# Second layer of a two-layer attention and expert kernel: the last group's expert rows scaled, added and put into statistics one batch per turn, its query block and the two blocks behind it one turn later

## The chip, the cores and the metric

One Trainium2 chip, one core. The metric is device time in microseconds (us) of one launch. The time before is 733.93 us, the median of 3 runs (733.39 to 734.78).

## What is computed

The input `x` is 16 batches of 112 tokens with 256 features, the context 375 rows of 256 features per batch. Two layers follow one another, each of cross attention and a feed-forward part, each part on a layer norm of `x` and added to `x`:

```
x = x + _L0_xattn_ref(_layernorm(x), ctx, ctx, mask, ...)   # one head, masked, own layer norm
x = x + _L0_ffn_ref(_layernorm(x), ...)                     # top 2 of 8 experts and 2 shared ones
x = x + _L1_xattn_ref(_layernorm(x), ctx, ctx, Wq, Wk, Wv, Wo)
x = x + _L1_ffn_ref(_layernorm(x), W, b, V_r, C)            # x @ (W + C V_r^T) + b
```

`_L1_xattn_ref` has 16 heads of 16 features:

```
scores = jnp.einsum('bhqd,bhkd->bhqk', q, k) * scale
attn = jax.nn.softmax(scores, axis=-1)
ctx = jnp.einsum('bhqk,bhkd->bhqd', attn, v)
return ctx.transpose(0, 2, 1, 3).reshape(...) @ Wo.T
```

## The kernel before

The 16 batches are four groups `i` of four batches `j`. The first layer's attention and shared experts come first, then 35 tiles of 128 expert rows (up to about 516 us), then the second layer. The result of the experts lies in DRAM (`yscr`). For each batch the two rows of every token are gathered into `yg[:, j, k, :]` (`gather`, L1857, indirect DMA issued by GpSimd), weighted and added to `x_res`. Then come layer norm statistics (`row_stats`, `rows_joined`), the reciprocal root (`rstd_of`) and the normalized rows `xh`, of which the second layer's queries are made. Groups 0 to 2 go through this beside the expert tiles. The last group, 3, can be gathered only after the last tile, and goes through it inside the second layer's attention.

That attention runs in **turns** `b` = 0 to 14, written out by hand in `tensor`, `vector`, `scalar`, `gpsimd` and `sync` of `second_layer`, and a tail for batch 15. Turn `b` of TensorE computes, for batch `b`, the transposed scores in four quarters `q` of four heads, each in three chunks `k` of keys (`transposed`, L2371), and the product with the values (`outputs`, L2380). It also computes the plain scores of batch `b + 2`, eight pairs `g` of heads (`scores`, L2351), which serve only for the row maxima. The engines' shares of a turn are:

- VectorE: eight reductions (`maximum`, L1996), one per pair. Two of them (`g` = 0, 1) come first, then the heads of batch `b - 1` (`finish`, L2008, L2010), the copy of the transposed maxima of `b + 1` (`turned`, L2002), then `g` = 2 to 7. Scores use two pairs of PSUM banks in turn, so `scores(b, g)` waits until `maximum` has read the pair before the last one (`EARLIER`, `pair_read`).
- ScalarE: `keep_outputs(b - 1)` (L2208) and twelve exponentials (`exps`, L2204), three per quarter. `transposed(b, q + 1)` waits for the exponentials of quarter `q`, chunk by chunk, since they read its banks. `outputs` wait for them too.
- GpSimd: `parted(b)` (L1769 to L1775) splits the maxima of batch `b` into three bf16 parts. TensorE transposes them (`maxima_T`, L2356) in turn `b - 1`.
- SyncE: keys, values and the rows of maxima by DMA.

Some turns carry a **block** of the other work (`BLOCKS`): `q` the queries of group 3, `o` the output projection of a group and its residual and statistics, `f` the feed-forward product. A block of `q` and `f` needs its group normalized. GpSimd does that (`rstd_of`, `normalized_beside`, L1839 to L1847), between two `parted`.

For group 3 before the change: ScalarE scales the eight rows of `yg` in turns 2 and 3 (`scaled`, L2199, four in each turn). GpSimd adds them (`combine`, L1880), two batches and then two. VectorE does the four `bn_stats` (L1917) and four `bn_aggr` (L1928, L1930) in one go in turn 4, behind `turned(5)`. The `q` block stands in turn 5, `o` of group 0 in turn 6 and `f` of group 0 in turn 8. Turns 7, 9, 11 and 14 have no block.

Of the kernel before, what the change touches and what calls it, by code (L numbers as in the profile page):

```python
# [22 lines left out]
G = 4  # L23
NG = B // G
# [1593 lines left out]
def second_layer(nc, tensors, first, routed, dram, out, x_res, weight1, weight2, slots, mhalf, ps, bank, ident, new_semaphore, pool_semaphore):  # L1618
# [29 lines left out]
    EARLY = NG - 1  # L1648


    BLOCKS = {5: ("q", 3), 6: ("o", 0), 8: ("f", 0), 10: ("o", 1), 12: ("f", 1), 13: ("o", 2), 15: ("f", 2)}
    NORMALIZED = {4: ("q", 3), 7: ("f", 0), 11: ("f", 1), 14: ("f", 2)}

    def blocks_in(b):
        return BLOCKS.get(b, (None, None))

# [39 lines left out]
    def pair_bank(use, k):  # L1696
        return bank[2 * PAIR[use] + k]
# [49 lines left out]
    def split_queries(eng, i):  # L1747

        eng.wait_ge(s["q1_ready"], (i + 1) * C)
        if i:  # L1750
            eng.wait_ge(s["q_out"], i * 16)
        eng.tensor_copy(qa[:, 1, :, :], qr[:]).then_inc(s["q2_ready"], 1)
        eng.wait_ge(s["q2_ready"], 3 * i + 1)
        eng.tensor_tensor(qr[:], qr[:], qa[:, 1, :, :], ALU.subtract).then_inc(s["q2_ready"], 1)
# [117 lines left out]
    def gpsimd(pool, n):  # L1872

        def combine(i, js):
            for j in js:
                for k in range(2):
                    pool.wait_ge(s["scaled"], 2 * j + k + 1)
                    if k:
                        pool.wait_ge(s["added"], 2 * j + k)
                    pool.tensor_tensor(x_res[:, i * G + j, :], x_res[:, i * G + j, :], yg[:, j, k, :], ALU.add).then_inc(s["added"], 1)  # L1880

        ones_below(pool, 1)
        ones_below(pool, 2)
        ones_below(pool, 3)
        pool.memset(va[:, :, :, :, HD:HD + 1], 1.0).then_inc(s["va_ready"], 1)
        pool.wait_ge(s["va_ready"], 2)
        zeros_below(pool, 1)
        pool.wait_ge(s["m_ready"], 4)
        split_queries(pool, EARLY - 1)
        split_rest(pool, EARLY - 1)  # L1890
        i = NG - 1
        for j in range(G):
            if j % 2:
                parted(pool, j // 2 + 2)
            pool.wait_ge(s["p_ready"], (2 * j + 2) * NKC)
            gather(pool, i, j)
        for j in range(0, G, 2):
            combine(i, range(j, j + 2))
            parted(pool, j // 2 + 4)
        rstd_of(pool, n, NORMS["q", i])  # L1900
        normalized_beside(pool, i, NORMS["q", i])
        parted(pool, 6)
        parted(pool, 7)
        split_queries(pool, i)
        split_rest(pool, i)
        for i, batches in enumerate(((8,), (9, 10, 11, 12), (13, 14, 15))):
            for b in batches:
                parted(pool, b)
            rstd_of(pool, n, NORMS["f", i])
            normalized_beside(pool, i, NORMS["f", i])  # L1910
            add_bias(pool, i)
        i = NG - 1
        rstd_of(pool, n, NORMS["f", i], AHEAD)
# [6 lines left out]
    def mean_var(v, n, i, js=slice(0, G)):  # L1920
        row_stats(v, n, i, js)
        rows_joined(v, n, js)
# [65 lines left out]
    def vector(v, n):  # L1988
# [71 lines left out]

        for b in range(B - 1):
            what, i = blocks_in(b)
            kind, k = NORMALIZED.get(b, (None, None))
            ahead_of = b + 2 < B
            if ahead_of:
                maximum(b + 2, 0)
                maximum(b + 2, 1)
            if b:
                finish(b - 1)
            turned(b + 1)  # L2070
            if kind == "q":
                v.wait_ge(s["added"], 2 * G)
                mean_var(v, n, k)
            if ahead_of:
                for g in range(2, 5):
                    maximum(b + 2, g)
            if ahead_of:
                maximum(b + 2, 5)
                maximum(b + 2, 6)
            if what == "o":  # L2080
                attended(i, slice(0, 2))
                v.wait_ge(s["x3_ready"], i * G + 2)
                row_stats(v, n, i, slice(0, 2))
                attended(i, slice(2, G))
            elif what == "f":
                results(i)
            if ahead_of:
                maximum(b + 2, 7)
            if what == "o":
                v.wait_ge(s["x3_ready"], i * G + G)  # L2090
                row_stats(v, n, i, slice(2, G))
                rows_joined(v, n)

        finish(B - 2)
        i = NG - 1
# [73 lines left out]
    def scalar(a):  # L2169
        A = nc.scalar.activation  # L2170

        def late_values(b):
            lo, hi = late_banks(b)
            a.wait_ge(s["v_ps"], b + 1)
            A(va[:, b - NV, 0:2, :, 0:HD], bank[lo][0:KC, :].rearrange("p (c h d) -> p c h d", c=2, d=HD), ACT.Copy)
            A(va[:, b - NV, 2, :, 0:HD], bank[hi][0:KC, 0:D].rearrange("p (h d) -> p h d", d=HD), ACT.Copy).then_inc(s["v_ready"], 1)

        def turned_over(what, i):
            for c in range(C):
                chunk_out(a, what, i, c, pair_bank(("over", what, i), c))  # L2180

        def ahead_turned(k, banks):

            for c in range(C):
                a.wait_ge(s["T_ps"], TAIL + k + c + 1)
                A(xhL[:, c, 0:AHEAD.stop * S], banks[c][:, 0:AHEAD.stop * S], ACT.Copy).then_inc(s["T_ready"], 1)

        def last_turned(k):

            a.wait_ge(s["T_ps"], TAIL + k + 1)  # L2190
            A(xhL[:, :, AHEAD.stop * S:GS], bank[6][:, 0:C * S].rearrange("p (c t) -> p c t", c=C), ACT.Copy).then_inc(s["T_ready"], 1)

        def scaled(b, n):

            if 2 <= b < 4:
                i = NG - 1
                j, k = divmod(4 * (b - 2) + n, 2)
                a.wait_ge(s[f"y_in{j}"], (i + 1) * 32)
                A(yg[:, j, k, :], yg[:, j, k, :], ACT.Copy, scale=(weight1, weight2)[k][:, i * G + j:i * G + j + 1]).then_inc(s["scaled"], 1)  # L2199

        def exps(b, q, ks=range(NKC)):
            for k in ks:
                a.wait_ge(s["st_ps"], (b * 4 + q) * NKC + (k + 1))
                A(pT[:, q % 2, k, :], bank[4 + k][0:KC, 0:QUAD * S], ACT.Exp).then_inc(s["p_ready"], 1)  # L2204

        def keep_outputs(b):
            a.wait_ge(s["pv_ps"], b + 1)
            A(outT[:].rearrange("p q t -> p (q t)"), bank[7][:, 0:GS], ACT.Copy).then_inc(s["outT_ready"], 1)  # L2208

        for c in range(C):  # L2210
            chunk_out(a, "q", EARLY - 1, c, bank[7 - 2 * c])
        late_values(NV)
        load_keys(a, 2)
        for m in range(C):
            query_out(a, EARLY - 1, m, bank[7 - 2 * m])
        late_values(NV + 1)
        late_values(NV + 2)
        load_queries(a, 1)
        late_values(NV + 3)
        late_values(NV + 4)  # L2220
        load_keys(a, 3)

        A(outT[0:1, 0, 0:1], mhalf[0:1, 0:1], ACT.Exp)
        late_values(NV + 5)
        store_queries(a, EARLY - 1)
        for b in range(B - 1):
            what, i = blocks_in(b)
            if b:
                keep_outputs(b - 1)
            exps(b, 0)  # L2230
            exps(b, 1)
            scaled(b, 0)
            exps(b, 2, range(1))
            scaled(b, 1)
            if what is not None:
                turned_over(what, i)
            exps(b, 2, range(1, NKC))
            scaled(b, 2)
            exps(b, 3, range(1))
            scaled(b, 3)  # L2240
            if what == "q":
                for m in range(C):
                    query_out(a, i, m, pair_bank(("product", what, i), m))
            exps(b, 3, range(1, NKC))
            if b == G + 2:
                store_queries(a, NG - 1)

        b = B - 1
        keep_outputs(b - 1)
        exps(b, 0)  # L2250
        turned_over("f", NG - 2)
        exps(b, 1)
        ahead_turned(0, AHEAD_BANKS["o"])
        exps(b, 2)
        exps(b, 3)
        keep_outputs(b)

        A(half[0:1, :], mhalf[0:1, 0:1], ACT.Sqrt, scale=-1.0)
        last_turned(2)
        ahead_turned(3, AHEAD_BANKS["f"])  # L2260
        a.wait_ge(s["rstd_ready"], MV + NORMS["f", NG - 1] + 2)
        A(root[:], half[:], ACT.Sqrt, scale=-2.0).then_inc(s["root_ready"], 1)
        last_turned(5)
        results_out(a, NG - 1, AHEAD)
# [442 lines left out]
```

## Time and profile before

| | |
|---|---|
| time, median of 3 runs | 733.93 us (733.39 to 734.78) |
| the profiled execution: its time, its span | 736.22 us, 734.4 us |
| mean granted TensorE clock | 0.997 |
| busy share TensorE, VectorE, ScalarE, GpSimd | 98%, 64%, 42%, 37% |
| second layer's turns 1 to 14 | about 558 to 705 us |

The page names PE for TensorE, DVE for VectorE, ACT for ScalarE, POOL for GpSimd, and SP for SyncE; PEld are TensorE's weight loads. An instruction's row gives its start, its duration, engine, line and tiles, and in brackets how long its engine stood idle before it and what ended that. Matmul rows of one line that follow one another are put into one row, whose time reaches to the end of the last. Turns are told apart below by the start of the transpose L2356, of which there is one per turn: window `b` runs from that of turn `b` to that of turn `b + 1`. Instructions that stand behind `turned(b + 1)` in the code lie in window `b`, and those ahead of `keep_outputs(b - 1)` in window `b - 1`.

### The profile page before, as it was taken

Reading aid. Unit: us, or ns where it says so; the run is one execution under the profiler, and the core shown is the slowest. Engines: PE = TensorE matmul, PEld = TensorE weight load, DVE = VectorE, ACT = ScalarE, POOL = GpSimd, SP = SyncE. Lnnn points to the kernel's source line nnn. Section 1 sums busy time; section 2 is a strip of 40 time slices with the busy share of each in tenths; the row PEclk is TensorE's granted clock in tenths of the full one; section 3 lists DMA queues with packets and bytes.
Section 4 is the critical chain, followed back from the end, with each engine's and each line's share of the span. In section 5 each row is a group of like instructions: output and inputs, shape, how many; then the busy total and the mean of one; then the engine's idle time right before and its main releaser. Section 6 shows DMA issues by size and latency. Waiting matters only on the chain.

```text
span 734.4 us, 15558 instructions
## 1 busy us (share of the span) xinstructions
PE 721.7 (98%) x5770; PEld 559.1 (76%) x5770; DVE 470.8 (64%) x1074; ACT 312.0 (42%) x559; POOL 269.4 (37%) x318
## 2 busy tenths in 40 slices
PE   8999999999999999999999999999999999999998
PEld 6686668766776575699999998989777667777776
DVE  4778674657465679644444565838678877788735
ACT  1224222421142122155555555554236755565563
POOL 4985333523320534402200514223734434405050
PEclk9999999999999999999999999999999999999999
DMA  9799943741521496822353423353886675764101
GB/s 254 200 299 265 239 139 130 217 126 42 174 86 53 133 376 202 295 68 84 108 144 103 117 74 98 122 152 121 244 240 180 178 209 148 204 180 116 40 4 51
DMA packets 73516, 114.10 MB, mean 155 GB/s; under 512 B 15153, under 2 KB 59794, under 8 KB 71522
## 3 DMA queue, kind: packets, MB, share of 16 engines
q1 hardware_dynamic: 61984, 85.93, 40.6%
q0 software_dynamic: 6160, 15.67, 6.8%
q10 hardware_dynamic: 5298, 11.51, 5.5%
q8 instruction: 47, 0.77, 0.5%
q14 instruction: 27, 0.22, 0.1%
HBM read 84.27 MB, written 28.41 MB: 153 GB/s over the span
## 4 chain that ended last, share of the span: by engine, by line
PE 88%; DVE 3%; POOL 3%; ACT 2%; DMA 2%; issue 1%; ACTq 0%; DVEq 0%; SPq 0%
PE ps L1587 17%; PE ps L1204 12%; PE ps L1596 8%; PE ps L1224 6%; PE ps L2380 6%; PE ps L2351 5%; PE ps L1243 5%; PE ps L2371 4%; PE ps L1255 4%; PE ps L1172 3%; PE ps L2344 3%; PE ps L1144 2%; PE ps L2325 2%; PE ps L1179 2%; PE ps L2280 2%; DVE mxh L1996 1%
## 5 line engine op out<-in xcount | busy, mean ns | idle before, releaser
L1996 DVE TENSOR_REDUCE mxh<-ps 112x2 f32<-112x750 f32 x128 | 115.3, 933 | 31.0 <-PE ps L2351 28.4
L1587 PE MATMUL ps<-rowsT,w 128*128 128x128 f32 x1120 | 130.9, 275 | 0.0
L1587 PEld LDWEIGHTS ps<-rowsT,w 128*128 128x128 f32 x1120 | 128.0, 192 | 0.2
L2204 ACT ACTIVATE d_pT<-ps 125x448 f32<-125x448 f32 x192 | 91.7, 550 | 43.2 <-PE ps L2371 41.2
L1541 ACT ACTIVATE w<-rw 128x1024 f32 x70 | 73.8, 1056 | 64.7 <-PE ps L1587 56.3
L1204 PE MATMUL ps<-x1T,sw 128*128 128x448 f32 x256 | 101.3, 540 | 0.0
L1204 PEld LDWEIGHTS ps<-x1T,sw 128*128 128x128 f32 x256 | 47.5, 190 | 38.5 <-issue 35.1
L1480 POOL DMA_DIRECT2D yscr<-y x35 | 19.7, 563 | 152.9 <-DVE y L1514 152.9
L1596 PE MATMUL ps<-rw,h 128*128 x280 | 66.4, 380 | 0.0
L2351 PE MATMUL ps<-kst,qst 96*112 96x375 bf16 x256 | 59.0, 335 | 1.3 <-DVE mxh L1996 1.2
L995 ACT ACTIVATE silu<-ps,sb 128x448 f32<-128x448 f32 x32 | 20.3, 633 | 87.0 <-PE ps L1204 87.0
L1596 PEld LDWEIGHTS ps<-rw,h 128*128 128x128 f32 x280 | 50.7, 191 | 6.8 <-issue 1.4
L2371 PE MATMUL ps<-qst,kst 128*128 128x112 bf16 x768 | 53.2, 214 | 0.3 <-ACT d_pT L2204 0.2
L2371 PEld LDWEIGHTS ps<-qst,kst 128*128 128x128 bf16 x768 | 43.3, 98 | 11.4 <-issue 4.5
L1224 PE MATMUL ps<-sw,gluT 128*128 128x256 f32 x224 | 50.7, 379 | 0.0
L1499 DVE TENSOR_TENSOR h<-ps,rb 128x512 f32<-128x512 f32 x35 | 24.1, 689 | 37.1 <-PE ps L1587 37.1
L1224 PEld LDWEIGHTS ps<-sw,gluT 128*128 128x128 f32 x224 | 42.1, 190 | 6.7 <-issue 0.4
L1503 DVE TENSOR_TENSOR h<-ps,rb 128x512 f32<-128x512 f32 x35 | 24.2, 691 | 32.1 <-PE ps L1587 32.1
L388 POOL DMA_INDIRECT xg<-xh_moe,places x32 | 31.5, 984 | 26.0 <-PE ps L1204 18.0
L558 DVE SCALAR_TENSOR_TENSOR gluT<-ps,sb,silu 128x448 f32<-128x448 f32 x32 | 21.8, 681 | 28.5 <-ACT silu L995 28.0
L1857 POOL DMA_INDIRECT yg<-yscr,slots x32 | 31.1, 972 | 23.4 <-ACT d_pT L2204 13.6
L2351 PEld LDWEIGHTS ps<-kst,qst 96*112 96x112 bf16 x256 | 25.3, 131 | 14.6 <-issue 5.2
(272 smaller groups left out, 1205.1 us busy)
## 6 DMA issues: line engine op xcount, KB each, us to landing
kst<-kscr SPq DMA_DIRECT2D x39, 378.0 KB, 5.4
rw<-in_rw SPq DMA_DIRECT2D x24, 512.0 KB, 9.1
kscr<-ka SPq DMA_DIRECT2D x16, 567.0 KB, 3.8
cT<-in_ctx_t SPq DMA_DIRECT2D x17, 378.0 KB, 4.9
ctxT<-in_ctx_t SPq DMA_DIRECT2D x16, 378.0 KB
ctxn<-in_ctx SPq DMA_DIRECT2D x16, 336.0 KB
rows<-xg SPq DMA_DIRECT2D x35, 128.0 KB, 2.7
rb<-in_rb SPq DMA_DIRECT2D x35, 128.0 KB, 3.1
```

Source lines behind the costliest of these rows:

```text
L388: pool.indirect_dma_start(out=dram["xg"], out_offset=bass.IndirectOffsetOnAxis(ap=places[0:S, k, b:b + 1], axis=0), in_=xh_moe[:, b, :], i ...
L1204: last = mm(bank[up_in(i, m)[k]][:, 0:GS], (sw1, sw2)[k][:, e, c, h * P:(h + 1) * P], x1T[:, c, :], start=c == 0, stop=c == C - 1)
L1224: last = mm(bank[down_in(i, j)][:, 0:D], gluT[:, m, j * P:(j + 1) * P], sw3[:, e, h, :], start=m == 0, stop=m == U - 1)
L1243: last = mm(ps[:, 2 + m, 0:KP], wk1[:, c, m * P:(m + 1) * P], context_T(b)[:, c, :], start=c == 0, stop=c == C - 1)
L1541: A(w12[:, k, :, :], (rw1, rw2)[k][:, e, :, :], ACT.Copy).then_inc(s[("w1_ready", "w2_ready")[k]], 1)
L1587: last = mm(bank[1 + 2 * q + k][:, block], w12[:, k, c, block], rowsT[:, q, c * P:(c + 1) * P], start=c == 0, stop=c == C - 1)
L1596: last = mm(y_bank(n)[:, 0:D], h2[:, q, m * P:(m + 1) * P], rw3[:, e, m, :], start=m == 0, stop=m == HM - 1)
L1996: V.tensor_reduce(mxh[:, b % 2, 2 * g:2 * g + 2], ps[0:S, p:p + 2, 0:K], axis=AX_X, op=ALU.max).then_inc(s["s_max"], 1)
L2204: A(pT[:, q % 2, k, :], bank[4 + k][0:KC, 0:QUAD * S], ACT.Exp).then_inc(s["p_ready"], 1)
L2351: last = mm(pair_bank(("score", b, g), k)[0:S, 0:K], qst[i % 2][0:DEPTH, h, j * S:(j + 1) * S], kst[b % 4][0:DEPTH, h, 0:K], start=True, s ...
L2371: last = mm(bank[4 + k][:, h * S:(h + 1) * S], kst[b % 4][:, QUAD * q + h, k * KC:k * KC + P], qst[i % 2][:, QUAD * q + h, j * S:(j + 1) * ...
L2380: last = mm(bank[7][32 * h:32 * h + HD + 1, q * S:(q + 1) * S], values[:, k, QUAD * q + h, :], pT[:, q % 2, k, h * S:(h + 1) * S], start=k ...
```

## The change

`scaled` now runs in turns 1 to 4, two per turn, for batch `j = b - 1`. The first comes at the head of the turn, ahead of `keep_outputs`, and the second between the exponentials of quarters 1 and 2. GpSimd adds batch 0 between the gathers of batches 2 and 3, then batch 1, then batches 2 and 3, each behind one `parted`. VectorE does one `bn_stats` in each of turns 2 to 5 behind `turned`, and the four `bn_aggr` in turn 5. The `q` block goes from turn 5 to 6, `o` of group 0 from 6 to 7, `f` of group 0 from 8 to 9. The query store of group 3 goes with them.

```diff
-    BLOCKS = {5: ("q", 3), 6: ("o", 0), 8: ("f", 0), 10: ("o", 1), 12: ("f", 1), 13: ("o", 2), 15: ("f", 2)}
-    NORMALIZED = {4: ("q", 3), 7: ("f", 0), 11: ("f", 1), 14: ("f", 2)}
+    BLOCKS = {6: ("q", 3), 7: ("o", 0), 9: ("f", 0), 10: ("o", 1), 12: ("f", 1), 13: ("o", 2), 15: ("f", 2)}
+    SUMMED = 2
...
             gather(pool, i, j)
-        for j in range(0, G, 2):
-            combine(i, range(j, j + 2))
-            parted(pool, j // 2 + 4)
+            if j == 2:
+                combine(i, range(1))
+        for j in range(1, G):
+            combine(i, range(j, j + 1))
+            parted(pool, j + 3)
         rstd_of(pool, n, NORMS["q", i])
         normalized_beside(pool, i, NORMS["q", i])
-        parted(pool, 6)
         parted(pool, 7)
+        parted(pool, 8)
         split_queries(pool, i)
         split_rest(pool, i)
-        for i, batches in enumerate(((8,), (9, 10, 11, 12), (13, 14, 15))):
+        for i, batches in enumerate(((9,), (10, 11, 12), (13, 14, 15))):
...
             turned(b + 1)
-            if kind == "q":
-                v.wait_ge(s["added"], 2 * G)
-                mean_var(v, n, k)
+            if SUMMED <= b < SUMMED + G:
+                j = b - SUMMED
+                v.wait_ge(s["added"], 2 * (j + 1))
+                row_stats(v, n, NG - 1, slice(j, j + 1))
+                if j == G - 1:
+                    rows_joined(v, n)
...
-            if 2 <= b < 4:
-                i = NG - 1
-                j, k = divmod(4 * (b - 2) + n, 2)
+            if 1 <= b <= G:
+                i, j, k = NG - 1, b - 1, n
                 a.wait_ge(s[f"y_in{j}"], (i + 1) * 32)
...
+            scaled(b, 0)
             if b:
                 keep_outputs(b - 1)
             exps(b, 0)
             exps(b, 1)
-            scaled(b, 0)
+            scaled(b, 1)
             exps(b, 2, range(1))
-            scaled(b, 1)
             if what is not None:
                 turned_over(what, i)
             exps(b, 2, range(1, NKC))
-            scaled(b, 2)
             exps(b, 3, range(1))
-            scaled(b, 3)
...
-            if b == G + 2:
+            if b == G + 3:
                 store_queries(a, NG - 1)
```

ScalarE's order from the end of turn 0 to the middle of turn 2, before (the `yg` rows are `scaled`, `d_pT` the exponentials, `outT` `keep_outputs`):

```order
435 L2204 ACTIVATE d_pT<-ps 125x448 x12
436 L2208 ACTIVATE outT<-ps 128x448
437 L2204 ACTIVATE d_pT<-ps 125x448 x12
438 L2208 ACTIVATE outT<-ps 128x448
439 L2204 ACTIVATE d_pT<-ps 125x448 x6
440 L2199 ACTIVATE yg<-yg,weight 112x256
441 L2204 ACTIVATE d_pT<-ps 125x448
442 L2199 ACTIVATE yg<-yg,weight 112x256
443 L2204 ACTIVATE d_pT<-ps 125x448 x2
```

and after the change (its L2202, L2207, L2211 are the same three statements):

```order
435 L2207 ACTIVATE d_pT<-ps 125x448 x12
436 L2202 ACTIVATE yg<-yg,weight 112x256
437 L2211 ACTIVATE outT<-ps 128x448
438 L2207 ACTIVATE d_pT<-ps 125x448 x6
439 L2202 ACTIVATE yg<-yg,weight 112x256
440 L2207 ACTIVATE d_pT<-ps 125x448 x6
441 L2202 ACTIVATE yg<-yg,weight 112x256
442 L2211 ACTIVATE outT<-ps 128x448
```

The first scaled row now stands ahead of the `outT` copy of turn 1; no turn has more than two, and none stands between two exponentials of one quarter.

VectorE's order in turn 4 before (`mxh` are the maxima; the first row is the end of `turned(5)`):

```order
684 L2002 COPY mT<-ps 48x112
685 L1917 BN_STATS d_stat<-x_res 112x6 x4
686 L1928 BN_AGGR d_mv<-d_stat 112x2 x3
687 L1930 BN_AGGR d_mv<-d_stat 112x2
688 L1996 TENSOR_REDUCE mxh<-ps 112x2 x8
```

and in turns 4 and 5 after the change:

```order
686 L2004 COPY mT<-ps 48x112
687 L1919 BN_STATS d_stat<-x_res 112x6
688 L1998 TENSOR_REDUCE mxh<-ps 112x2 x8
689 L2010 RECIPROCAL rec<-ps 112x16
690 L2012 TENSOR_TENSOR heads<-ps,rec 112x256
691 L2004 COPY mT<-ps 48x112
692 L1919 BN_STATS d_stat<-x_res 112x6
693 L1930 BN_AGGR d_mv<-d_stat 112x2 x3
694 L1932 BN_AGGR d_mv<-d_stat 112x2
695 L1998 TENSOR_REDUCE mxh<-ps 112x2 x8
```

Turns 2 and 3 have one `BN_STATS` at the same place as turn 4. The aggregation moved one turn down.

GpSimd's order around the last two gathers, as a piece of the difference:

```order
 L1857 DMA yg<-yscr,slots 112x256 x4
+L1880 TENSOR_TENSOR x_res<-x_res,yg 112x256 x2
 L1769 CAST mparts<-mxh 112x16
 L1771 TENSOR_TENSOR mr<-mxh,mparts 112x16
```

The addition of batch 0 now stands ahead of `parted(3)` and of the gather of batch 3.

## Rows read from the trace of the kernel before

**Rows 1.** The page: span.
```profile
span 734.4 us, 15558 instructions
```

**Rows 2.** Busy time by window, windows 1 to 5 and 7: length, then each engine.
```profile
core 0: us, PE busy (x) PEld busy (x) DVE busy (x) ACT busy (x) POOL busy (x), PEclk, DMA share, GB/s
558.56:567.57 9.01, 9.01 (x167) 6.42 (x166) 8.03 (x12) 6.10 (x14) 4.60 (x9) 1.00 0.80 220
567.57:576.99 9.42, 9.22 (x167) 6.51 (x166) 7.99 (x12) 7.56 (x18) 5.31 (x10) 1.00 0.78 203
576.99:586.40 9.41, 9.21 (x166) 6.51 (x165) 7.98 (x12) 7.55 (x18) 3.75 (x8) 1.00 0.67 166
586.40:596.70 10.30, 9.38 (x167) 6.54 (x166) 9.37 (x20) 6.11 (x14) 6.92 (x10) 1.00 0.84 233
596.70:609.87 13.17, 13.05 (x182) 8.77 (x182) 8.12 (x12) 8.06 (x18) 1.93 (x6) 1.00 0.68 175
...
623.72:632.72 9.00, 9.00 (x166) 6.41 (x165) 8.11 (x12) 5.95 (x13) 8.47 (x13) 1.00 0.81 221
```

**Rows 3.** Timeline of turn 2: ScalarE around the scaled rows, TensorE behind them.
```profile
570.02 0.54 ACT L2204 ACTIVATE d_pT<-ps 125x448 f32<-125x448 f32 x1 [0.89 <-PE ps L2371]
570.46 0.50 ACT L2199 ACTIVATE yg<-yg,weight 112x256 f32<-112x256 f32 x1
570.86 0.53 ACT L2204 ACTIVATE d_pT<-ps 125x448 f32<-125x448 f32 x1
571.68 0.97 ACT L2204 ACTIVATE d_pT<-ps 125x448 f32<-125x448 f32 x2
571.65 0.99 PE L2371 MATMUL ps<-qst,kst 128*128 128x112 bf16 x12
```

**Rows 4.** Timeline of turn 1, which has no scaled rows: the same place.
```profile
561.01 1.42 ACT L2204 ACTIVATE d_pT<-ps 125x448 f32<-125x448 f32 x3 [0.89 <-PE ps L2371]
563.05 1.85 ACT L2204 ACTIVATE d_pT<-ps 125x448 f32<-125x448 f32 x4 [0.63 <-issue]
562.65 0.76 PE L2371 MATMUL ps<-qst,kst 128*128 128x112 bf16 x12
```

**Rows 5.** Timeline of turn 4: VectorE's statistics, TensorE's scores behind them.
```profile
587.14 0.20 DVE L2002 COPY mT<-ps 48x112 bf16<-48x112 bf16 x1
587.27 1.39 DVE L1917 BATCH_NORM_STATS2 d_stat<-x_res 112x6 f32<-112x256 f32 x4
588.86 3.43 DVE L1996 TENSOR_REDUCE mxh<-ps 112x2 f32<-112x750 f32 x4
589.81 0.53 PE L2351 MATMUL ps<-kst,qst 96*112 96x375 bf16 x2 [0.60 <-DVE mxh L1996]
590.65 0.53 PE L2351 MATMUL ps<-kst,qst 96*112 96x375 bf16 x2 [0.32 <-DVE mxh L1996]
```

**Rows 6.** Timeline of turn 2: VectorE without statistics.
```profile
568.31 0.20 DVE L2002 COPY mT<-ps 48x112 bf16<-48x112 bf16 x1
568.65 1.78 DVE L1996 TENSOR_REDUCE mxh<-ps 112x2 f32<-112x750 f32 x2
```

**Rows 7.** Timeline, turn 0 to 1: last gather of batch 0; `keep_outputs(0)` and its reader.
```profile
553.74 0.96 POOL L1857 DMA_INDIRECT yg<-yscr,slots  x1 [0.30 <-issue]
557.21 0.54 ACT L2208 ACTIVATE outT<-ps 128x448 f32<-128x448 f32 x1 [1.27 <-PE ps L2380]
558.02 0.60 PE L2389 MATMUL ps<-ident,outT 128*112 128x128 f32 x4
```

**Rows 8.** Gathers, tile `yg`: from issue to landing, that one alone, then all measured.
```profile
DMA to landing us min/median/max: 3.0/3.0/3.0
...
DMA to landing us min/median/max: 3.0/3.7/4.8
```

**Rows 9.** Timeline of GpSimd, turns 4 to 5: normalization of group 3, then `parted(6)`.
```profile
589.02 0.23 POOL L1839 TENSOR_SCALAR d_rstd<-d_mv 112x4 f32<-112x4 f32 x1 [3.70 <-DVE d_mv L1930]
596.15 0.22 POOL L1775 TENSOR_TENSOR mparts<-mr,mparts 112x16 bf16<-112x16 f32 x1
```

More of the change, by code:

```diff
@@ L2062, in vector @@
             what, i = blocks_in(b)
-            kind, k = NORMALIZED.get(b, (None, None))
             ahead_of = b + 2 < B
```

## The prediction

> **What bounds the kernel now.** I read the windows of the second layer first, since the change touches nothing ahead of them. In a window without a block, TensorE is busy for 9.01 of 9.01 us (window 1) and 9.00 of 9.00 (window 7) [rows 2]: the turn is as long as TensorE's own work. VectorE has 8.03 us in it and ScalarE 6.10, so each has room, but only at the right place. Three windows without a block are longer: 2 with 9.42 us, 3 with 9.41, 4 with 10.30 [rows 2]. The excess over 9.01 is 0.41 + 0.40 + 1.29 = **2.10 us**, and these are the three windows in which group 3 is scaled (2, 3) and put into statistics (4). This is all that the change can win; on a span of 734.4 us [rows 1] it is 0.29%. The window with the `q` block takes 13.17 us at 13.05 busy [rows 2], about its work as well.
>
> The timeline then says why. In turn 2, ScalarE puts a scaled row between exponentials, each 0.40 us from its start to the next start (570.46 to 570.86) [rows 3]. Two of them lie ahead of the exponentials that start at 571.68, and TensorE's twelve transposed-score matmuls stretch to 0.99 us [rows 3] from the 0.76 of turn 1 [rows 4]. In turn 4, VectorE's statistics start at 587.27 and the next reduction starts at 588.86; TensorE's scores wait 0.60 and 0.32 us for it [rows 5].
>
> **The change, part by part.** Δ is against the profiled execution.
>
> 1. *Scaled rows out of turns 2 and 3, two per turn.* The first sits at the head of a turn, where ScalarE idled 1.27 us ahead of `keep_outputs` [rows 7]; 0.40 us fits. The second delays the two exponentials of quarter 2 behind it by 0.40 us. Undisturbed, the three of turn 1 start at 561.01, the third ends at 562.43, and ScalarE then idles 0.63 us [rows 4]. Its reader is the last third of the twelve matmuls that start at 562.65 and take 0.76 us [rows 4], so from about 563.0 on. The delayed end is 562.83: 0.2 us early. So two per turn cost nothing, where four cost 0.4. Δ = −0.41 − 0.40 = −0.81. From the other side: if the 0.2 us were not there, each of four turns would lose at most 0.40.
>
> 2. *Statistics out of turn 4.* Before, the next reduction stood at 588.86, which is 1.72 us behind the copy of 587.14 [rows 5]. Without statistics it stands 0.34 us behind (568.31 to 568.65) [rows 6]. So the shift was 1.38 us and the window grew by 1.29: about **0.09 us of a shift is free**. Δ = −1.29.
>
> 3. *One `bn_stats` in each of turns 2, 3, 4.* It starts 0.13 us behind the copy (587.14 to 587.27) and four of them take 1.39 us [rows 5]. I take each as a step of 0.33 us (the last one overlaps what follows, so a quarter of 1.39 less a little). The reduction then stands 0.46 us behind the copy instead of 0.34, since 0.15 to 0.2 us of that gap was idle anyway: a shift of 0.12, less the free 0.09, makes 0.03 per turn. Δ = +0.1. Bounds: 0, and the whole quarter, 0.35 each, 1.05 together.
>
> 4. *The last `bn_stats` and four `bn_aggr` in turn 5.* Of the 1.59 us from 587.27 to 588.86 three steps of 0.33 go, 0.60 stays, on top of the 0.13. The reduction stands 0.73 behind the copy, a shift of 0.39, less 0.09. Δ = +0.3. Bounds: 0 and 0.60.
>
> 5. *GpSimd.* Its eight additions stay as many and hide as before: the statistics of batch `j` in turn `j + 2` want an addition done in turn `j + 1`, over 2 us earlier. The normalization now starts in turn 5 and `parted(7)` is queued behind it. Before, this chain ran from 589.02 to 596.37, 7.35 us, and TensorE's transpose came at 596.70 [rows 2, 9]. Now it starts about 0.9 us behind the copy of turn 5 (0.73, and 0.16 from the last reduction's place to `rstd`), and ends 8.25 behind. The transpose came 8.68 us behind the copy in window 2 (568.31 to 576.99) [rows 2, 6], so 8.27 in a window of 9.01, and 8.6 in this one, which is 0.3 longer. It just fits: 0, with 0.1 to 0.3 us at stake if the start is later.
>
> 6. *The blocks one turn later.* Turn 5 becomes plain, turns 6, 7 and 9 carry what 5, 6 and 8 did. The blocks keep their neighbours on GpSimd: a plain turn for normalization between `o` and `f` of group 0. On SP, the results of group 0 now stand ahead of the keys of batch 13 instead of 12, which are needed a turn later too. The load of group 3's queries stays in SP's turn 8, with the store now one turn before it, not two. They are read by the scores of batch 12 in turn 10, all of turn 9 later, at least 9 us. Δ = 0. If the cover failed, a wait would stand at turn 10.
>
> 7. *The wait moved to turn 1.* This is the one new exposure. The scaled row at the head of turn 1 waits for both gathers of batch 0; before, it was not wanted until turn 2. Behind it on ScalarE are `keep_outputs(0)` and all exponentials of turn 1, and TensorE waits for both. The second gather is issued at 553.74 and lands 3.0 us later, at 556.74 [rows 7, 8]. The scaled row then holds ScalarE until 557.2, and `keep_outputs(0)` started at 557.21, ending at 557.75, with its reader at 558.02 [rows 7]: 0.27 us to spare. So Δ = 0, by a hair. Bounds: 0, and by the longest landing of a gather, 4.8 us [rows 8], 1.5 us.
>
> Here a page speaks against the change. The Trainium skill ("DMA: Bandwidth & Descriptors", section "Latency and other measured facts") says that the wait for memory, the main part of a DMA's fixed cost, is 0.2 us on average and 2 us at high load. By its figures a landing could come 1.8 us later than the best, an estimate, and take back most of the gain. The landings of 3.0 to 4.8 us [rows 8] spread just as widely; the one that counts was the quickest.
>
> **Sum:** −0.81 − 1.29 + 0.1 + 0.3 = **−1.7 us**. The profiled execution took 736.22 us, 2.29 over the median, and 1.82 over its own span; I take the difference as it is to the median: 733.93 − 1.7 = **732.2 us**.
>
> **Rivals.**
>
> A. *VectorE has less room than the 0.09 suggests.* VectorE has 8.03 of 9.01 us, and a `bn_stats` of 0.35 in three turns and 0.60 in the fourth could all pass into the turn: 1.65 us back. Then 2.10 − 1.65 = 0.45 saved, 733.5 us. For it: with statistics in turn 4, nearly all of the shift was paid. Against: the gap behind the copy holds idle time that swallows most of a single one.
>
> B. *The gather of batch 0 is late.* At 4.8 us it lands at 558.54, the scaled row ends its 0.40 at 558.94, and `keep_outputs` starts 1.73 us late, less 0.27: 1.46 us back, −0.24, so 733.7 us. Half of that at the middle landing of 3.7: −1.3. For it: it is the quickest of the landings, and the wait is exposed. Against: nothing ahead of 553.74 changes, so the same transfer meets the same traffic.
>
> C. *Slower.* The same place, as a mechanism of its own: `yg` arrives after a landing so long that all exponentials of turn 1 stand. TensorE is late by the landing less 3.34 us (557.21 + 0.27 − 0.40 − 553.74). The gain is gone at a landing of 5.0 us, and from 6.5 us on the kernel is over 0.2% slower; at 7.1 us it gives 736.0 us. No gather here took over 4.8.
>
> D. *The change does not do what it says:* the excess of windows 2 to 4 would belong to something else, the keys' DMAs or GpSimd. Then the time stays, 733.9. Against: the waits in brackets name ScalarE's exponentials and VectorE's maxima, and the plain windows 1 and 7, with the same DMAs of keys, have 9.01 and 9.00 [rows 2].
>
> **How the numbers follow.** 0.2% is 1.47 us, about what a measurement of this kernel can tell from no change. The forecast is worth 1.7, close above it. Forecast (a saving of 1.5 to 2.1): 0.57. A, in part or whole (0.4 to 1.4): 0.20. B: 0.14. D, and a late `parted(7)` or query load that eats part of it: 0.04. C, or another wait over 3 us: 0.05. Faster 0.57, same 0.38, slower 0.05. The range goes from the full 2.10 and 0.2 of measurement (731.6) to rival A whole (733.6); above it lie C, D and the late end of B.
>
> **What would show it.** Right: windows 2 and 3 at 9.0 to 9.1 us, window 4 at 9.0 to 9.1, window 5 (plain now) at about 9.3, the `q` window 13.2, all others as they were. Wrong, A: windows 2 to 4 at 9.3, window 5 at 9.6, and scores (L2352 there) that wait for maxima. Wrong, B or C: ScalarE's `outT` of turn 1 released by a DMA or behind a late `yg` row, window 0 or 1 longer. Wrong on GpSimd: the transpose of turn 6 waits for `mparts`.

## The result, and the profile after

The change makes the kernel slower. Over 8 runs of each, the changed kernel takes 737.52 us (736.38 to 741.56), the kernel before 734.85 (733.39 to 735.90). The ratio is 1.0043, with a 95% interval of 1.0031 to 1.0055, or 2.3 to 4.0 us. The forecast was 1.7 us faster. The profiled execution is near the quick end of its runs: 736.95 us, with a span of 735.1. That of the kernel before was a long one (736.22 us), so the two spans do not show the loss: its window 0 took 11.31 us with TensorE's clock granted at 0.85, against 10.17 at 1.00 here.

By windows, as [rows 2], windows 1 to 8 (window 6 is the `q` block now, 7 is `o` of group 0, 9 is `f`):

```profile
558.14:567.14 9.00, 9.00 (x166) 6.41 (x165) 8.01 (x11) 6.87 (x16) 5.61 (x11) 1.00 0.79 217
567.14:576.20 9.06, 9.06 (x167) 6.46 (x166) 8.23 (x13) 6.89 (x16) 4.58 (x9) 1.00 0.73 195
576.20:585.26 9.06, 9.06 (x167) 6.47 (x166) 8.23 (x13) 6.88 (x16) 2.26 (x6) 1.00 0.69 181
585.26:595.76 10.50, 9.21 (x166) 6.39 (x166) 8.23 (x13) 6.49 (x15) 1.57 (x5) 1.00 0.85 224
595.76:606.41 10.65, 9.24 (x166) 6.49 (x165) 8.45 (x16) 6.10 (x14) 6.94 (x10) 1.00 0.95 239
606.41:619.58 13.17, 13.05 (x183) 8.77 (x182) 8.13 (x12) 8.07 (x18) 1.94 (x6) 1.00 0.40 111
619.58:633.42 13.84, 13.65 (x190) 10.12 (x189) 10.83 (x24) 7.33 (x17) 6.47 (x9) 1.00 0.44 131
633.42:642.63 9.21, 9.17 (x167) 6.34 (x166) 8.14 (x12) 5.96 (x14) 8.52 (x13) 1.00 0.85 226
```

Windows 2 and 3 did what was forecast: 9.06 us each instead of 9.42 and 9.41. Windows 4 and 5 are 10.50 and 10.65 us long, with TensorE busy for only 9.21 and 9.24. The last two columns show where to look: the DMA engines are busy 0.85 and 0.95 of these windows, at 224 and 239 GB/s. The share alone proves nothing, since window 4 of before had 0.84 [rows 2]. The timeline of TensorE and SyncE shows both waits:

```profile
588.06 0.58 SPq L1788 DMA_DIRECT2D vt<-vscr  x1
588.74 2.99 SPq L2138 DMA_DIRECT2D qst<-qscr  x3
591.78 1.86 SPq L1728 DMA_DIRECT2D kst<-kscr  x3
594.64 0.75 PE L2372 MATMUL ps<-qst,kst 128*128 128x112 bf16 x12 [1.29 <-issue]
603.77 0.53 PE L2352 MATMUL ps<-kst,qst 96*112 96x375 bf16 x2 [1.26 <-DMA kst<-kscr]
```

In turn 4 SyncE issues the values of batch 5 (`vt`), the queries of group 2 (`qst`, three parts) and the keys of batch 8 (`kst`, three parts). The view of DMA issues gives the size of each and its time to landing, here for the values, the third part of the queries and the third part of the keys:

```profile
vt<-vscr SPq DMA_DIRECT2D x1, 408.0 KB, 6.5
...
qst<-qscr SPq DMA_DIRECT2D x1, 448.0 KB, 8.7
...
kst<-kscr SPq DMA_DIRECT2D x1, 378.0 KB, 10.7
```

The values land at 588.06 + 6.5 = 594.56 us. TensorE, idle since 593.35, goes on at 594.64. The bracket of that row names no releaser ("issue"). In the code the wait for the values of batch 5 stands right ahead of these matmuls, and in each of the seven profiles that have this wait TensorE starts 0.09 us after the values landed. The matmuls themselves read only queries and keys; the first product that reads the values, `outputs(5, 0)`, starts at 597.10, 2.5 us later. The keys land at 593.04 + 10.7 = 603.7 (the third of the three issues starts at 593.04), and the first scores of batch 8 start at 603.77.

Before, the same transfers were hidden. The third part of those keys was issued at 595.48, and the scores of batch 8 came in turn 6, behind the 13.17 us of window 5 [rows 2]:

```profile
593.45 2.62 SPq L1728 DMA_DIRECT2D kst<-kscr  x3
607.22 0.53 PE L2351 MATMUL ps<-kst,qst 96*112 96x375 bf16 x2
```

```profile
kst<-kscr SPq DMA_DIRECT2D x1, 378.0 KB, 8.9
```

They landed at 604.4, 2.8 us ahead of the 607.22. The change took the 4.16 us of the `q` block (13.17 − 9.01) out of this turn: 2.8 − 4.16 makes 1.4 us late, and the trace shows a wait of 1.26.

### The profile page after: what moved, and what is told of

It reads as the page before. It is cut to its first block, busy times and chain, and to the rows that moved or that the text cites. A ratio compares the mean times of both kernels' runs of the same rounds, so it can differ in the third digit from the quotient of the medians.

```text
span 735.1 us, 15558 instructions
## 1 busy us (share of the span) xinstructions
PE 719.5 (98%) x5770; PEld 557.0 (76%) x5770; DVE 469.8 (64%) x1074; ACT 312.4 (42%) x559; POOL 270.2 (37%) x318
## 4 chain that ended last, share of the span: by engine, by line
PE 83%; DMA 5%; DVE 4%; POOL 3%; issue 2%; ACT 1%; SPq 1%; ACTq 0%; DVEq 0%
PE ps L1587 17%; PE ps L1204 12%; PE ps L1596 8%; PE ps L1224 6%; PE ps L2381 5%; PE ps L2352 5%; PE ps L2372 4%; PE ps L1243 4%; PE ps L2345 3%; PE ps L1255 2%; PE ps L1172 2%; PE ps L1144 2%; PE ps L2326 2%; PE ps L2281 2%; DMA kscr<-ka 2%
## 5 line engine op out<-in xcount | busy, mean ns | idle before, releaser
L2207 ACT ACTIVATE d_pT<-ps 125x448 f32<-125x448 f32 x192 | 91.4, 549 | 42.1 <-PE ps L2372 41.0
L2352 PEld LDWEIGHTS ps<-kst,qst 96*112 96x112 bf16 x256 | 24.8, 129 | 15.2 <-issue 5.0
```

The costliest lines, as they stand in the source:

```text
L2352: last = mm(pair_bank(("score", b, g), k)[0:S, 0:K], qst[i % 2][0:DEPTH, h, j * S:(j + 1) * S], kst[b % 4][0:DEPTH, h, 0:K], start=True, s ...
```

## The experiments

Twelve kernels were run, five rounds each beside the kernel before. e1 to e4 ran on one chip. e5, e6, e7 and e10 ran on a second one and e8, e9, e11 and e12 on a third, where the kernel before took 738.8 and 739.3 us instead of 734.2. In all profiles from these two, window 0 is 11.2 us (9.75 to 10.30 in e1 to e4), window 1 is 10.7 to 12.8 (9.0 to 9.3) and window 2 is 9.4 to 9.8. So times are compared by their ratio to before, taken beside it on the same chip; between chips even the ratios are a rough guide. In e3, e9 and e11 half of some loads is left out, so that they compute with what an earlier batch left there. Three theories were tested: **T**, the transfers above; **R1**, the scaled row that waits for the first gather at the head of turn 1; **R2**, the statistics one batch per turn.

### e1: only the blocks later

```diff
-    BLOCKS = {5: ("q", 3), 6: ("o", 0), 8: ("f", 0), 10: ("o", 1), ...}
-    NORMALIZED = {4: ("q", 3), 7: ("f", 0), ...}
+    BLOCKS = {6: ("q", 3), 7: ("o", 0), 9: ("f", 0), 10: ("o", 1), ...}
+    NORMALIZED = {5: ("q", 3), 8: ("f", 0), ...}
```

(with GpSimd's `parted` and the query store moved to fit.)

> The kernel before with one part of the change alone: the q block, and o and f of group 0, one turn later, with the statistics in one go in turn 5; the scaled rows stay four per turn in turns 2 and 3. Theory T (transfers): the long turn 5 gave the values and keys that are loaded beside the queries of group 2 the time to land; with turn 5 plain they arrive late. Then windows 2 and 3 stay 9.4 us, windows 4 and 5 are over 10 us both, and the time is 3 to 5 us over before, slower than the changed kernel by about 1. Rival R1 (the new place of the scaled rows, the gather of batch 0 first): this kernel equals before within 0.5 us, since that place is not in it. Rival R2 (statistics one batch per turn): also equal to before.

Measured: ratio 1.0050 (1.0033 to 1.0067), 737.13 against 734.15 us. Windows 4 and 5:

```profile
584.58:594.88 10.30, 9.17 (x167) 6.35 (x166) 8.03 (x12) 6.10 (x14) 0.83 (x4) 1.00 0.85 227
594.88:605.40 10.52, 9.44 (x166) 6.53 (x165) 9.39 (x19) 6.09 (x14) 6.92 (x10) 1.00 0.86 226
```

The loss in time is there with neither the new place of the scaled rows nor the spread statistics, so R1 and R2 fall as its cause. Window 4 has the late values (1.13 us of wait, and no statistics any more). Window 5 is long mainly for another reason: the statistics stand there now, and the same work made window 4 of before 10.30 us. No wait for the keys shows there. The profiled execution is the quickest of the six (735.95 us).

### e2: only the spreading, blocks as before

The lines added to the kernel before, without GpSimd's:

```diff
+    SUMMED = {2: (0,), 3: (1,), 4: (2, 3)}      # turn: batches put into statistics
...
+            if n in {1: (0, 2), 2: (0, 1, 2), 3: (0, 1, 2)}.get(b, ()):
...
+            scaled(b, 0)
+            scaled(b, 1)
             if b:
                 keep_outputs(b - 1)
             exps(b, 0)
             exps(b, 1)
+            scaled(b, 2)
```

> The kernel before with the other part alone: all blocks where they were (q in turn 5), scaled rows two in turn 1 and three each in turns 2 and 3 (two at the head, one before quarter 2), statistics of batch 0 in turn 2, of batch 1 in turn 3, of 2 and 3 with the aggregation in turn 4. Theory T: windows 2 and 3 at 9.05, window 4 at 9.6 to 9.7, window 5 13.2 as before, time 1.3 to 1.5 us under before (half of that if the values of batch 5 come late, since they now are wanted 0.7 us earlier). Rivals R1 and R2: 2 to 4 us over before, as in the changed kernel.

Measured: ratio 0.9992 (0.9983 to 1.0001), 733.60 against 734.15 us. In the profile windows 2 to 5 are 9.05, 9.06, 9.65 and 13.17, as forecast. The time fell by 0.6 us, about half of the expected 1.3 to 1.5, and the interval touches no change. Window 0 accounts for most of what is missing: it is 10.30 us where e1 and e4, without a scaled row at the head of turn 1, have 9.75.

### e3: the changed kernel with fewer bytes

```diff
+        w = NH * KP // 2 if b in (8, 9) else NH * KP        # keys
...
+            w = NH * GS // 2 if i == 2 else NH * GS         # queries
```

Each copy then takes only the first `w` elements of a row.

> The changed kernel, with half of the bytes left out of the loads of group 2's queries and of the keys of batches 8 and 9 (heads 8 to 15 keep what an earlier batch left there). Theory T: windows 4 and 5 fall from 10.5 and 10.65 to 9.05 and 9.35, 2.7 us in the profile, and the time falls by 2.5 to 5 us, to 1 to 2 us under before. Rivals R1 and R2: the time stays at that of the changed kernel, 2.5 to 3.5 over before.

Measured: windows 4 and 5 are 9.41 and 9.32. The time is 734.17 us, ratio 1.0004 (0.9988 to 1.0020). The windows did what T said, 2.4 us of 2.7, and the time fell to that of before; the further 1 to 2 us did not come. In its profile windows 2 to 9 are together 1.1 us shorter than those of before (86.64 against 87.76), but windows 0 and 1 are 10.29 and 9.28, 0.8 us over the 9.75 and 9.01 of e1.

### e4: the first scaled row of turn 1 out of the way

```diff
-            scaled(b, 0)
+            if b != 1:
+                scaled(b, 0)
...
             exps(b, 1)
+            if b == 1:
+                scaled(b, 0)
```

> The changed kernel, with the first scaled row of turn 1 behind keep_outputs and the first six exponentials, beside the second one, so that the gather of batch 0 holds up nothing at the head of the turn. Theory T: as the changed kernel within 0.5 us. Rival R1 (that gather lands late in the timed runs, though not in the profile): 1.5 to 3 us faster than the changed kernel.

Measured: ratio 1.0062 (1.0049 to 1.0075), against the changed kernel's 1.0043: not faster, and by the ratios 1.4 us slower, a miss for the "within 0.5 us". So R1 is not the cause of the loss. But the wait is not free. In the changed kernel's profile the row waits 1.46 us for the gather, the `outT` copy follows at 556.92, and TensorE waits for it:

```profile
556.51 0.51 ACT L2202 ACTIVATE yg<-yg,weight 112x256 f32<-112x256 f32 x1 [1.46 <-DMA yg<-yscr,slots]
556.92 0.52 ACT L2211 ACTIVATE outT<-ps 128x448 f32<-128x448 f32 x1
557.59 0.62 PE L2390 MATMUL ps<-ident,outT 128*112 128x128 f32 x4 [0.25 <-ACT outT L2211]
```

Window 0, of the kernel before, of the changed kernel and of e4:

```profile
547.25:558.56 11.31, 10.94 (x165) 7.67 (x166) 8.77 (x11) 5.62 (x13) 3.10 (x7) 0.85 0.52 157
547.97:558.14 10.17, 9.56 (x165) 6.58 (x166) 8.82 (x11) 5.98 (x14) 3.58 (x7) 1.00 0.63 187
547.25:557.00 9.75, 9.38 (x165) 6.54 (x165) 8.81 (x11) 5.62 (x13) 3.15 (x7) 1.00 0.53 167
```

e4 saves 0.42 us there, as does e1 (9.75). It loses more in window 4 (11.19; its values took 7.2 us to land) and window 9 (15.23, see below).

### e5: the queries behind the keys

```diff
-            if b in (G, 2 * G):
-
-                sp.wait_ge(s["st_ps"], b * 4 * NKC)
-                load_queries(sp, b // G + 1)
...
             if b + 4 < B:
                 sp.wait_ge(s["st_ps"], (b + 1) * 4 * NKC)
                 load_keys(sp, b + 4)
+            if b in (G, 2 * G):
+                sp.wait_ge(s["st_ps"], b * 4 * NKC)
+                load_queries(sp, b // G + 1)
```

> The changed kernel, with the queries of groups 2 and 3 loaded behind the keys of the same turn instead of ahead of them. Theory T: the values of batch 5 and the keys of batch 8 land in time, so window 4 falls from 10.5 to 9.1 us; the queries of group 2 then come last and, after the same bytes, are as late for turn 6 as the keys were, so window 5 stays at 10.5 to 11 us. Time 1 to 1.5 us under the changed kernel. A rival (only the order of issue on SP matters, not the bytes): both windows fall, time 2.5 us or more under the changed kernel.

Measured: ratio 1.0062 (1.0046 to 1.0079), slower than the changed kernel's ratio where 1 to 1.5 us less was expected. Window 4 fell to 9.06 us, as expected: the values land after 4.7 us. Window 5 rose to 15.51:

```profile
589.06:598.12 9.06, 9.06 (x167) 6.47 (x166) 8.22 (x13) 6.50 (x15) 1.57 (x5) 1.00 0.67 181
598.12:613.63 15.51, 10.75 (x167) 7.50 (x166) 8.47 (x17) 6.43 (x15) 6.93 (x10) 0.89 0.95 234
609.47 0.63 PE L2351 MATMUL ps<-kst,qst 96*112 96x375 bf16 x2 [4.62 <-DMA qst<-qscr]
610.03 1.32 PE L2380 MATMUL ps<-d_pT,vt 125*17 125x112 f32 x24
```

The queries can be issued only behind the keys, which wait for the end of turn 4, so they start later than before as well as being last. TensorE's clock fell behind the 4.62 us of idle time: it was granted 0.89 over this window, which is 3.4 us at the lower level (1.2 GHz) from 609.70 on, and the product behind the wait took 1.32 us instead of 0.77.

### e6 and e7: the spread kernel with the queries behind the keys, and with a statistic moved

e6 is e2 with the edit of e5 for group 2 alone. e7 has this besides:

```diff
-    SUMMED = {2: (0,), 3: (1,), 4: (2, 3)}
+    SUMMED = {2: (0,), 3: (1,), 4: (3,)}
...
                 maximum(b + 2, 5)
+                if b == 3:
+                    v.wait_ge(s["added"], 6)
+                    row_stats(v, n, NG - 1, slice(2, 3))
                 maximum(b + 2, 6)
```

> The kernel e2_spread_q5 with the queries of group 2 loaded behind the keys of batch 8. Theory T: turn 5 with its q block is 13.2 us long and leaves them the time, all windows as in e2 and time equal to e2 within 0.3 us, with the runs closer together, since the values of batch 5 no longer share the queues with the queries. Rival: the queries come too late for turn 6, window 5 over 13.5 us, and the time over that of e2.

> As e6, with the statistics of batch 2 in turn 3, behind the maximum of pair 5, where VectorE waited 0.3 us for scores. By the reading that a shift of a reduction is free up to 0.09 us and VectorE's gaps swallow the rest, window 3 stays at 9.05 to 9.2 and window 4 falls from 9.65 to 9.3 us; time 0.2 to 0.3 us under e6, 1.5 under before.

Measured: e6 0.9982 (0.9971 to 0.9994), e7 0.9985 (0.9971 to 0.9999). Their windows 4 are 9.65 and 9.32, the statistic in VectorE's gap costs nothing (window 3 stays 9.05), and windows 5 are 13.46 and 13.24, so the queries come a little late there: 0.29 us of e6's gain, 0.07 of e7's. e7 was expected 1.5 us under before; its ratio makes 1.1.

### e10: only `o` and `f` of group 0 later

```diff
-    BLOCKS = {5: ("q", 3), 6: ("o", 0), 8: ("f", 0), 10: ("o", 1), ...}
+    BLOCKS = {5: ("q", 3), 7: ("o", 0), 9: ("f", 0), 10: ("o", 1), ...}
```

> The kernel before with only o and f of group 0 one turn later (turns 7 and 9; q stays in turn 5, turn 6 and turn 8 are plain; scaled rows and statistics as before). It separates the two query loads: that of group 3 now meets the plain turn 8, that of group 2 the long turn 5 as before. Theory T, if both loads count: windows 0 to 5 as before, windows 8 or 9 0.2 to 1.6 us longer (the changed kernel had 9.20, the variant e4 9.21 and 15.23), time 0.2 to 1.8 us over before. If only group 2's load counts: as before within 0.3 us.

Measured: ratio 1.0000 (0.9990 to 1.0010), windows 8 and 9 9.01 and 13.59. The move of these two blocks alone is free. What costs is the `q` block's leaving turn 5.

### e8, e9 and e11: the changed kernel again, and with half of one load

e8 is the changed kernel; e9 and e11 have one of the two edits of e3 each, half of the queries of group 2 and half of the keys of batches 8 and 9.

> The changed kernel itself once more, so that the three below and it are timed on one chip in the same rounds. Expected: 2 to 4 us over before, windows 4 and 5 over 10 us.

> The changed kernel, with half of the bytes of group 2's queries left out (heads 8 to 15 keep those of group 0). Those bytes stand beside the values of batch 5 and ahead of the keys of batch 8. Theory T: window 4 falls to 9.1 to 9.6 and window 5 to about 9.4 us; time 1.5 to 3 us under the changed kernel. If the bytes of the keys themselves are the cause, it stays within 0.7 us of it.

> The changed kernel, with half of the bytes of the keys of batches 8 and 9 left out. Theory T: those keys are issued behind the values of batch 5, so window 4 stays at 10 us or more, and window 5 falls to about 9.4; time 0.7 to 1.8 us under the changed kernel.

| | time | ratio to before (95%) | windows 4, 5 |
|---|---|---|---|
| e8 | 741.42 us | 1.0029 (1.0010 to 1.0048) | 10.49, 10.50 |
| e9, half queries | 738.79 us | 0.9989 (0.9976 to 1.0003) | 9.86, 9.31 |
| e11, half keys | 739.45 us | 1.0008 (0.9992 to 1.0023) | 10.55, 9.32 |

Each load's share is read off window by window. With half of the keys, only window 5 recovers, since the values of batch 5 are issued ahead of them. With half of the queries, which stand between the two, both recover, window 4 less than expected (9.86, not 9.1 to 9.6). The time follows: 2.6 and 2.0 us under e8.

These three and e4 show one more loss: window 9 takes 15.2 us instead of 13.6. In e8:

```profile
637.04:646.26 9.22, 9.22 (x167) 6.52 (x166) 8.13 (x12) 5.97 (x14) 8.51 (x13) 1.00 1.01 264
646.26:661.49 15.23, 13.84 (x191) 10.18 (x190) 9.54 (x16) 7.08 (x16) 0.83 (x4) 1.00 0.60 157
652.11 0.38 PE L2381 MATMUL ps<-d_pT,vt 125*17 125x112 f32 x6 [1.28 <-issue]
```

TensorE stands idle from 650.83 to 652.11, after 18 of the 24 matmuls of one product, where no semaphore is waited for. In all four profiles it stops at this same matmul, and each time a transfer on the instruction queue (16 KB) ended 0.1 to 0.3 us before: here it ran from 649.31 to 650.58. The view of DMA queues for 645 to 653 us has it:

```profile
q1 hardware_dynamic: 296, 1.81, 91.2%
q8 instruction: 1, 0.02, 1.0%
```

In these four the transfer starts 22 or 23 matmuls ahead of that place; in the other four profiles with `q` in turn 6 (the changed kernel's first, e1, e3, e5) it starts 50 to 90 matmuls ahead, and TensorE does not stop. So TensorE most likely waits for its own instructions, though the profile does not name the engine that they are for. Window 8 has the DMA engines busy 0.98 to 1.01 in the four and 0.80 to 0.95 in the others; that this makes the transfer late is not shown.

### e12: the spread kernel, a statistic moved, the loads as before

This is e2 with e7's edit of the statistics, without that of the queries.

> The kernel e2_spread_q5 (blocks as before, scaled rows and statistics spread), with the statistics of batch 2 in turn 3 behind the maximum of pair 5; the queries are loaded where they were. Window 4 at 9.32, window 5 at 13.2, time 1.0 to 1.7 us under before.

Measured: 736.93 against 739.32 us, ratio **0.9965 (0.9952 to 0.9979)**, 1.6 to 3.5 us under before, where 1.0 to 1.7 were expected: faster than both kernels. Windows 2 to 5:

```profile
568.57:577.98 9.41, 9.16 (x166) 6.50 (x165) 8.22 (x13) 7.37 (x17) 4.28 (x10) 1.00 0.74 196
577.98:587.04 9.06, 9.06 (x166) 6.47 (x165) 8.56 (x14) 6.49 (x15) 2.95 (x7) 1.00 0.68 171
587.04:596.36 9.32, 9.17 (x166) 6.49 (x165) 8.43 (x17) 6.09 (x14) 6.91 (x10) 1.00 0.88 230
596.36:609.53 13.17, 13.05 (x183) 8.77 (x182) 8.12 (x12) 8.06 (x18) 1.94 (x6) 1.00 0.78 199
```

Window 4 has the DMA engines as busy as in the changed kernel (0.88), and window 5, with the `q` block, takes up what is left. Windows 2 to 4 are 27.79 us together; in e10, the one profile with the statistics of before and the same longer windows 0 and 1, they are 29.53. That is 1.7 us of the gain.

## Why the prediction was wrong

- **Step 1, scaled rows: right.** Forecast 9.0 to 9.1 us for windows 2 and 3, measured 9.06, 9.06. On the two other chips window 2 stays at 9.4 to 9.5 in the spread kernels, and is 9.82 in e10, whose scaled rows stand as before.
- **Steps 2 to 4, statistics: right, to a few hundredths.** One `bn_stats` behind `turned` was to cost 0.03 us per turn and costs about 0.05 (9.05 or 9.06 against 9.01). The last one with the aggregation was to cost 0.3: window 5 is 9.31 or 9.32 once its transfers are lightened (e9, e11). Window 4 is 9.06 where nothing waits for the values (e5). Rival A, VectorE with less room, is out.
- **Step 5, `parted(7)`: right.** The chain ends in time; no transpose waits for `mparts`.
- **Step 7, the wait for the gather: wrong by a small amount.** It said "Δ = 0, by a hair". The gather landed 2.7 us after its issue (553.80 to 556.51), as quickly as forecast, and yet window 0 is 10.17 us instead of the 9.75 of e1 and e4: 0.4 us. The 0.27 us to spare had been read in a window 0 that took 11.31 us, with 3.4 us of it at TensorE's lower clock; there TensorE starts the last product that the `outT` copy waits for 2.6 us behind the gather's issue (556.37 against 553.74), in the changed kernel, at the full clock, only 1.7 us behind it (555.52 against 553.80). B, whose mechanism this is, forecast 0.4 to 1.5 us for landings of 3.7 to 4.8 (its "half of that" at 3.7 is a slip: 0.36 of 1.46 is a quarter, and its −1.3 is right). C is out. The Trainium skill ("DMA: Bandwidth & Descriptors", section "Latency and other measured facts") gives 0.2 us on average and 2 us at high load for the wait for memory, by which the landing could have come 1.8 us later, an estimate; for this transfer no run shows that.
- **Step 6, the blocks one turn later: this is the step that failed.** It said "Δ = 0" after looking only at what else stands in the blocks' turns and at the queries of group 3. It did not ask what the `q` block was covering. Turn 5 was the one long turn between the loads of turn 4 (408 KB of values, three parts of 448 KB of queries, three of 378 KB of keys, 2.9 MB) and the first scores that read those queries and keys. Made plain, it gives them 4.16 us less. The values are not under that cover, since TensorE waits for them at the head of turn 5, ahead of the block; their lateness is a second, separate loss that came with the move. In place of 0 stand +1.4 us in window 4 (10.50 against 9.06), +1.3 in window 5 (10.65 against 9.32) and +0.2 in window 8, whose cause is open (e1 and e3 have 9.00 there). So the forecast −1.7 becomes +1.3 over windows 2 to 9 (89.09 us against 87.76 before). With the 0.4 of window 0 that is 1.7 in the profiled execution, whose time is 2.1 over the median of before. In some executions there are 1.6 more in window 9, 3.3 in all; the timed difference is 2.3 to 4.0.
- The late keys could have been counted from the trace of before: landed 604.4, wanted 607.2, and 4.16 us taken away. The late values could not be foreseen so. Before, they landed 2.3 us ahead of the matmuls that wait for them, and the shortened window 4 takes 1.24 of that, so 1 us should have been left:

```profile
589.21 0.58 SPq L1788 DMA_DIRECT2D vt<-vscr  x1
vt<-vscr SPq DMA_DIRECT2D x1, 408.0 KB, 4.1
595.57 0.75 PE L2371 MATMUL ps<-qst,kst 128*128 128x112 bf16 x12
```

- They take 6.5 us to land instead of 4.1. The kernels with a plain turn 5 and the queries behind the values have 5.4 to 7.2 us (seven of them, the changed kernel among them); those with the `q` block in turn 5 have 3.4 to 5.0 (before, e2, e6, e7, e10, e12). The trace narrows the cause. A load counts as landed when all of its sixteen parts are done. In every profile fifteen parts of these values are done 3.2 to 3.8 us after the issue; in the changed kernel the sixteenth comes at 6.5. In the seven late kernels a 16 KB transfer on the instruction queue starts 1.1 to 2.2 us after the issue, ahead of most of the values' bytes. In the six others it starts 2.7 us after it or later. The view of DMA queues for the 2.6 us behind the issue (588.06 to 590.66 us) shows it in the changed kernel, and for the same stretch of the kernel before (589.21 to 591.81) it has no such line:

```profile
q8 instruction: 1, 0.02, 3.4%
```

- The queries have their share too: with half of their bytes the values land after 5.4 and 5.8 us (e3, e9), and with none right behind them after 4.7 (e5), though all three have the early instruction transfer. No run moves the instruction transfer by itself, so its share is argued from the order of events, and why it starts earlier in these kernels stays open.
- The rival for the slower side had a DMA that lands late as its mechanism, but looked for it in the one wait that the diff adds, at turn 1. The loss came from waits that the diff does not touch.

## What to carry to other kernels

A block of compute that makes one stage long is also time in which transfers land. When it is moved, list every load in flight across the stage it leaves, take its landing and its first use from the trace, and subtract the block's length from the difference. Here 2.8 us to spare less 4.16 foretold the wait for the keys (1.26 us measured). Look also at where a wait stands: the values' wait stands 2.5 us ahead of their first reader, and moved down to it, it would have found them landed in the changed kernel (594.56 against 597.10); no run tried that. And here the gain on the engines could be had without the move: spread over the earlier turns, with the `q` block left in place, the kernel is 0.35% faster than before (e12), where with the block moved the kernel is 0.43% slower.

## What the runs showed of the hardware

- TensorE's clock fell after an idle wait of 4.62 us for a DMA (granted 0.89 over the window, 3.4 us of it at the lower level, the product behind it at 1.32 us instead of 0.77), so a late load costs more than its wait (e5).
- The time to landing is not the transfer's own: 408 KB of values took 3.5 to 7.2 us when 1.3 MB of queries were issued behind them on the same queue, and 3.4 to 5.0 when the keys stood between (e5, e6, e7). The load waits for the slowest of sixteen parts: fifteen were done within 3.8 us everywhere, and where the last came at 5.4 us or later a 16 KB instruction transfer had started ahead of most of the values' bytes.
- TensorE can stand idle in the middle of a run of matmuls with no wait in it, 1.28 us here, and goes on 1.4 to 1.5 us after a 16 KB instruction transfer has ended (e4, e8, e9, e11, four of the eight profiles in which the `q` block is in turn 6).
